# Graph attention layer on one core: where the adjacency chunks, the side jobs, the attribute sums and the projection stand in the order of a group

## The chip, the cores and the metric

The kernel runs on one NeuronCore of a Trainium2 chip. The metric is the device time of one execution in microseconds (us): the median of three runs before the change is 3267.39 us (3266.81 to 3270.06). The trace that is read here is of a separate, profiled execution.

## The reference, cut to what matters

```python
N, E = 6250, 200000                     # nodes, edges sorted by dst; 128 features, 4 heads
h  = relu(layernorm(x));  xp = h @ W
e  = leaky_relu(a_s[src] + a_d[dst]);   m = segment_max(e, dst)
w  = exp(e - m[dst])                    # softmax over the edges of a node, max subtracted
x  = x + relu(segment_sum(w/denom * xp[src], dst) + bias0)      # first layer
edge_agg = segment_sum(edge_attr @ We + be, dst)
x_comb   = concat([relu(layernorm(x)), edge_agg])
neigh    = segment_sum(x_comb[src], dst)                        # second layer
out = x + (relu((x_comb + neigh) @ W1 + b1) @ W2 + b2)
```

## The kernel before, in words

The edges are cut into 87 groups of 2304 (128 partitions x 18 columns). Every group `n` passes through an `item(n, ...)` on each of the five engines; a loop over pairs of groups runs most of them (`stage`). The items of the engines meet by semaphores only, so the order in which each engine's item is written is the order of the work.

What a group does on its main path: GpSimd (POOL) gathers the 18 columns of node rows by indirect DMA into `V` (`gather`, L906). VectorE (DVE) takes the logits, scans them (`pre1`), TensorE (PE) transposes the tails of the 128 partitions, DVE scans those (`tails`, L1835), PE brings them back (`cback`, L1298), DVE makes the running maxima and splits them into `peaks`. PE multiplies them with the group's selection matrix (`mg`, L1316: the peaks' product), DVE turns the result into the new maxima (`pen`, L1876, to `sh`), PE looks them up for every edge (`look`, L1332), DVE and ScalarE (ACT) form the weights (`lks` L1915, two exponentials), DVE multiplies the gathered rows (`vw`, L1932), and PE sums them into the window of 128 nodes (`sumV`, L1352, 36 instructions, 18 columns of two). Its last instruction signals `vm_b`; the end of it is called T in the text below. After T, SyncE (SP) may issue the attribute load of group n+2 (1152 KB) and then the load of `state`, which DVE's `rescale_state` of the next item (L1691) waits for.

Beside the main path each group has, on PE:

- `attribute_sums`: 18 columns of the edge attributes summed with the same selection in 32 bit (`SEL`, which ACT copies from the 16-bit one, `selc_b`), L1284, two instructions a column. Three columns stand ahead of the look-up, fifteen behind it.
- `adjacency`: 18 chunks of a dense adjacency for the second layer, L1253 and L1255. A chunk goes into one of three PSUM banks, and ACT copies it out into `adjE` (`keep_adjacency`, the ACTIVATE `xsb<-pt` and `xsb<-pa`, signal `ab_ev`). A chunk waits until the chunk three ahead of it has been copied out (`behind` 2 of `ab_ev`); ACT waits for PE by `ab_mm`, which is signalled for each third chunk and the last ones. When all 18 are out, SP stores 1176 KB (`store_adjacency`).
- the projection of a finished window (`transpose_window`, L1232 and L1233; ACT's copy `fhT`, `evacuate_window`; `project_window`, L1237 and L1238).
- in groups 39 to 83 a `job`: 14, 21 or 28 matmuls of 384 columns of the second layer (L1275), taken off the end of the kernel; DVE's `keep_job` (L1798) reads its result.

POOL's gather of 18 descriptors stops ahead of descriptor 11 until the peaks' product of the group before is there, and ahead of descriptor 14 until its look-up is there (`PAUSES`). Each of ACT's `keep_adjacency` calls first loads the chunks' places into registers (L1009).

PE's order in an item before the change: job part 1, tails' transpose, job part 2, `cback`, chunks 15 to 17 of group n-1, job part 3, peaks' product, chunks 0 to 2, attribute columns 0 to 2, look-up, chunks 3 to 5, attribute columns 3 to 17, transposes of window n-1, chunks 6 to 8, two thirds of `sumV`, projection of window n-1, last third of `sumV`, chunks 9 to 14. ACT's: `thruT`, chunks 15 to 17 of n-1, the copy of `SEL`, chunks 0 to 2, `fold` and the normalised window, chunks 3 to 5, the two exponentials of the weights, `fhT`, chunks 6 to 14.

Of the kernel before, what the change touches and what calls it, by code (L numbers as in the profile page):

```python
# [25 lines left out]
J = 18  # L26
# [66 lines left out]
FILL = (10, 14)  # L93


PAUSES = ((11, "mg_b"), (14, "look"))
# [19 lines left out]
def gnn_kernel(nc, x, src, dst, attr, W, att_src, att_dst, bias0, We, be, W1, b1, W2, b2, out):  # L116
    ctx = ExitStack()
    with ctx:
# [821 lines left out]
        def _(act):  # L940
# [94 lines left out]
            def item(n, b, it, like=0, is_extra=False):  # L1035
# [10 lines left out]
                if finish_before:  # L1046
                    keep_adjacency(n - 1, 1 - b, 15, 18)
# [4 lines left out]
                if not is_extra:  # L1052
                    after_dma(act, s("adj_out"), n - 1)
                    keep_adjacency(n, b, 0, 3)
                else:
# [8 lines left out]
                if not is_extra:  # L1064
                    keep_adjacency(n, b, 3, 6)
# [7 lines left out]
                if not is_extra:  # L1073
                    keep_adjacency(n, b, 6, 15)
# [5 lines left out]
            keep_adjacency(NG - 1, 0, 15, 18)  # L1080
# [41 lines left out]
        def _(pe):  # L1122
# [112 lines left out]
            def project_window(m):  # L1235
# [3 lines left out]
                if isinstance(m, int) and m == NG - 1:  # L1239
                    ins.then_inc(s("ym_f"), 1)  # L1240
# [21 lines left out]
            def job(n, like, lo, hi):  # L1262

                total = HP * parts_of(like)
                hi = min(hi, total)
                if lo >= hi:
                    return
                if lo == 0:
                    if isinstance(n, int):
                        pe.wait_ge(s("ys2"), parts_of(like))  # L1270
                    pe.wait_ge(s("aw_in"), n * 16 + (16 - JOB0 * 16))
                    pe.wait_ge(s("ab_ev"), n * J - (J - 15))
                for i in range(lo, hi):
# [3 lines left out]
                if hi == total:  # L1277
                    ins.then_inc(s("jb_mm"), 1)

            def item(n, b, it, like=0, is_extra=False):  # L1280
# [11 lines left out]
                job(n, like, 0, FILL[0])  # L1292
# [3 lines left out]
                job(n, like, FILL[0], FILL[1])  # L1296
# [3 lines left out]
                if finish_before:  # L1300
                    adjacency(n - 1, 15, 18)
# [10 lines left out]
                job(n, like, FILL[1], NB)  # L1312
# [5 lines left out]
                if not is_extra:  # L1318
                    adjacency(n, 0, 3, like)
# [4 lines left out]
                attribute_sums(0, 3)  # L1324
# [10 lines left out]
                if not is_extra:  # L1335
                    adjacency(n, 3, 6)
                attribute_sums(3, J)
# [6 lines left out]
                for q in range(QN):  # L1344
                    if q == QN - 1 and finish_before:
                        project_window(n - 1)
# [8 lines left out]
                if not is_extra:  # L1355
                    adjacency(n, 9, 15)
            stage(pe, item)
            adjacency(NG - 1, 15, 18)
# [86 lines left out]
        def _(dve):  # L1445
# [329 lines left out]
            def finish_projection(m):  # L1775

                if isinstance(m, int) and m == NG - 1:
# [307 lines left out]
```

## Time and profile before

| | us |
|---|---|
| median of 3 runs (lowest, highest) | 3267.39 (3266.81, 3270.06) |
| the profiled execution | 3249.53 |
| its span | 3247.6 |
| mean granted TensorE clock | 0.772 of full speed |
| PE busy, DVE busy, POOL busy, ACT busy | 2133.8, 1838.2, 1516.2, 1095.0 |

The span runs from the first instruction to the last one; the execution's own time lies 1.9 us above it. Groups 0 to 86 take it up to 2946.6 us, the second layer's tail the rest.

### The profile page before, as it was taken

To read this page: it belongs to the slowest core of one execution; us is meant where nothing else is said; L and a number is where in the kernel's file an instruction comes from. 1 tells how busy PE (TensorE), PEld (TensorE's weight loads), DVE (VectorE), ACT (ScalarE), POOL (GpSimd) and SP (SyncE) were. 2 spreads that over 40 slices of the span, in tenths; PEclk is the share of its full clock that TensorE was granted. 3 is DMA by queue.
4 is the path that set the end of the run, shared out by engine and by line. 5 is a ranking of instruction groups with operands and counts; after the bars stand their busy time and mean duration, and the time that the engine had idled before them with its cause. 6 is when DMAs were issued, how large, how long until landed. Compare 5 with 4: busy or idle time off the path is not lost.

```text
span 3247.6 us, 60418 instructions
## 1 busy us (share of the span) xinstructions
PE 2133.8 (66%) x16302; PEld 1640.0 (50%) x16302; DVE 1838.2 (57%) x6265; ACT 1095.0 (34%) x2343; POOL 1516.2 (47%) x1625
## 2 busy tenths in 40 slices
PE   4466665665666666656666676666676676667987
PEld 3354554554554545545445454454454445455766
DVE  7365666666666666656556565555555556564221
ACT  3333333333333344333333333333333233332000
POOL 3555555555555555554545555445444444550000
PEclk8666766766767766778878788788888788878999
DMA  9845545555555555565555655556555555655665
GB/s 195 121 137 163 167 139 163 155 153 162 155 153 163 148 165 172 152 182 150 179 153 174 173 170 180 149 162 177 159 153 176 166 147 172 180 138 189 209 198 159
DMA packets 395176, 532.44 MB, mean 164 GB/s; under 512 B 115603, under 2 KB 346723, under 8 KB 383665
## 3 DMA queue, kind: packets, MB, share of 16 engines
q1 hardware_dynamic: 344939, 415.35, 42.4%
q0 software_dynamic: 50112, 115.56, 15.9%
q8 instruction: 61, 1.00, 0.1%
q14 instruction: 64, 0.52, 0.1%
HBM read 385.48 MB, written 145.24 MB: 163 GB/s over the span
## 4 chain that ended last, share of the span: by engine, by line
PE 26%; DVE 21%; another core or an unknown queue 21%; issue 13%; DMA 8%; ACT 5%; SPq 5%; ACTq 1%; DVEq 1%
PE pv L1352 9%; PE pv L1284 5%; PE pt L1275 4%; ACT xsb L942 4%; DVE tabb L1640 4%; DMA state<-zpart 4%; DMA state<-sums 3%; PE pt L1253 2%; DVE big L1932 2%; PE pv L1409 2%; DVE lks L1915 1%; DVE fy L1759 1%; DVE fy L1768 1%; PE pt L1409 1%
## 5 line engine op out<-in xcount | busy, mean ns | idle before, releaser
L906 POOL DMA_INDIRECT big<-table,idx x1566 | 1489.2, 951 | 1372.4 <-issue 399.2
L942 ACT ACTIVATE xsb<-pt 128x343 f32 x1042 | 482.0, 463 | 1547.7 <-remote 922.0
L1253 PE MATMUL pt<-tabb 128*128 128x343 bf16 x1042 | 379.5, 364 | 448.1 <-ACT xsb L942 405.8
L1284 PE MATMUL pv<-big 128*128 128x128 f32 x3132 | 511.3, 329 | 8.0 <-issue 5.6
L1284 PEld LDWEIGHTS pv<-big 128*128 128x128 f32 x3132 | 476.3, 239 | 32.2 <-issue 13.7
L1352 PE MATMUL pv<-big 128*128 128x133 f32 x3132 | 391.6, 280 | 22.2 <-DVE big L1932 22.2
L1253 PEld LDWEIGHTS pt<-tabb 128*128 128x128 bf16 x1042 | 107.9, 104 | 553.8 <-ACT xsb L942 439.9
L1352 PEld LDWEIGHTS pv<-big 128*128 128x128 f32 x3132 | 367.9, 190 | 35.5 <-DVE big L1932 22.4
L1640 DVE TENSOR_TENSOR tabb<-pc,keyp 128x2064 bf16<-128x2064 bf16 x261 | 319.0, 1222 | 0.0
L942 ACT ACTIVATE xsb<-pa 128x343 f32 x521 | 240.9, 462 | 61.8
L1932 DVE TENSOR_TENSOR big<-big,pm 128x768 f32<-128x768 f32 x261 | 233.4, 950 | 30.8 <-ACT pm L942 19.0
L1255 PE MATMUL pt<-tabb 128*128 128x49 bf16 x1041 | 220.7, 212 | 0.0
L1691 DVE TENSOR_TENSOR state<-state,fold 128x128 f32<-128x128 f32 x87 | 25.5, 293 | 337.6 <-issue 205.1
L1253 PE MATMUL pa<-tabb 128*128 128x343 bf16 x521 | 187.3, 360 | 21.3 <-ACT xsb L942 20.6
L942 ACT ACTIVATE big<-selb 128x2304 f32<-128x2304 bf16 x87 | 183.9, 2114 | 2.6 <-issue 2.6
L1640 DVE TENSOR_TENSOR tabb<-pc,lop 128x768 bf16<-128x768 bf16 x261 | 144.3, 553 | 5.5
L1332 PE MATMUL pa<-node,selb 128*128 128x24 bf16 x1566 | 55.7, 179 | 139.5 <-DVE node L1674 59.3
L1275 PE MATMUL pt<-pro 128*128 128x384 bf16 x476 | 146.8, 492 | 0.0
L1275 PE MATMUL pt<-tabb,pro 128*128 128x384 bf16 x315 | 90.1, 447 | 84.6 <-ACT xsb L942 84.6
L1316 PE MATMUL pm<-peaks,selb 128*128 128x13 bf16 x1566 | 55.7, 173 | 122.6 <-remote 67.5
L1844 DVE SCALAR_TENSOR_TENSOR logit<-pm,cin,logit 128x4 f32<-128x4 f32 x87 | 19.3, 222 | 198.7 <-remote 180.6
L1332 PEld LDWEIGHTS pa<-node,selb 128*128 128x128 bf16 x1566 | 48.7, 101 | 158.3 <-DVE node L1674 65.3
(339 smaller groups left out, 3282.5 us busy)
## 6 DMA issues: line engine op xcount, KB each, us to landing
adj<-xsb SPq DMA_DIRECT2D x87, 1176.0 KB
big<-in_edge_attr_dram SPq DMA_DIRECT2D x87, 1152.0 KB
selb<-rel SPq DMA_DIRECT2D x87, 576.0 KB
pro<-adj SPq DMA_DIRECT2D x28, 896.0 KB
big<-table,idx POOLq DMA_INDIRECT x1566
state<-sums SPq DMA_DIRECT2D x87, 130.5 KB
sums<-state SPq DMA_DIRECT2D x87, 130.5 KB
pro<-adj SPq DMA_DIRECT2D x12, 672.0 KB
```

The lines of the kernel that those rows point to most:

```text
L906: pool.indirect_dma_start(out=V[b][:, j, 0:rows], out_offset=None, in_=table, in_offset=bass.IndirectOffsetOnAxis(ap=index[b][:, j:j + 1], ...
L942: return nc.scalar.activation(out_, in_, func, **kw).then_inc(s(name), 1)
L1253: ins = nc.tensor.matmul(to, ohl[:, c, :], ohk[:, c, 0:KW], start=True, stop=alone)
L1255: ins = nc.tensor.matmul(to.rearrange("p (q x) -> p q x", q=NPARTS)[:, :, 0:HP], ohl[:, (c - 1) % J, :], ohc[:, (c - 1) % J, 0:NB].rearran ...
L1275: ins = nc.tensor.matmul(jobP, jobT[:, q, :, h], yt[q][:, h, :], start=(i == 0), stop=(i == total - 1))
L1284: ins = nc.tensor.matmul(sumA[b], SEL[b][:, j, :], AT[b][:, j, :], start=(j == 0), stop=(j == J - 1))
L1316: ins = nc.tensor.matmul(mg, selH[:, j, :], peaks[:, j, :], start=(j == 0), stop=(j == J - 1))
L1332: ins = nc.tensor.matmul(lk[:, j, :], selT[:, j * 128:(j + 1) * 128], parts[b], start=True, stop=True)
L1352: ins = nc.tensor.matmul(sumV[b], SEL[b][:, j, :], V[b][:, j, 0:TAB], start=(j == 0), stop=(j == J - 1))
L1409: ins = nc.tensor.matmul(pay[k][0:rows, 0:NK * C], winT[k][:, q, 0:rows, h], yt[q][:, h, :], start=(i == 0), stop=(i == total - 1))
L1640: return v.tensor_tensor(to.rearrange("p j (w e) -> p j w e", e=2), v_in, at, ALU.is_equal)
L1932: v.tensor_tensor(v4, v4, wps[:, js, :].rearrange("p j (h a) -> p j h a", a=1) .to_broadcast([128, QUART, H, F]), ALU.mult).then_inc(s("vw ...
```

## The change

- `adjacency` and `keep_adjacency`: chunks 9 to 14 no longer follow `sumV`; with 15 to 17 they go into the next item, 9 to 14 behind `cback`, 15 to 17 behind the peaks' product. On ACT chunks 15 to 17 come behind the copy of `SEL`. Chunks 0 to 2 go from behind the peaks' product to behind the look-up; on ACT they stand where 3 to 5 stood, and 3 to 8 come behind `fhT`.
- `attribute_sums`: 9 columns ahead of the look-up in a group without a job, 3 in one with a job (`LEAD`), the rest behind chunks 0 to 2.
- `job`: in one piece, behind the leading attribute columns and ahead of the look-up; DVE reads it behind `edge_marks(n, 1)`.
- `project_window`: one item later, ahead of the tails' transpose; DVE's `finish_projection` waits for that transpose instead of `vm_b`.
- `PAUSES`: stops ahead of descriptors 9 and 12.

```diff
-FILL = (10, 14)
-PAUSES = ((11, "mg_b"), (14, "look"))
+PAUSES = ((9, "mg_b"), (12, "look"))
+LEAD = (9, 3)
...   ScalarE, item
                 a(thruT[:, :], thruP, ACT.Copy, "thru_c")
                 if finish_before:
-                    keep_adjacency(n - 1, 1 - b, 15, 18)
+                    keep_adjacency(n - 1, 1 - b, 9, 15)
                 after(act, s("sel_b"), n)
...
                 a(SEL[b], selH, ACT.Copy, "selc_b")
-                if not is_extra:
-                    after_dma(act, s("adj_out"), n - 1)
-                    keep_adjacency(n, b, 0, 3)
-                else:
+                if finish_before:
+                    keep_adjacency(n - 1, 1 - b, 15, 18)
+                if is_extra:
...
                 if finish_before:
                     normalise_window(n - 1)
                 if not is_extra:
-                    keep_adjacency(n, b, 3, 6)
+                    after_dma(act, s("adj_out"), n - 1)
+                    keep_adjacency(n, b, 0, 3)
...
                 if finish_before:
                     evacuate_window(n - 1)
                 if not is_extra:
-                    keep_adjacency(n, b, 6, 15)
+                    keep_adjacency(n, b, 3, 9)
...   TensorE, item
-                job(n, like, 0, FILL[0])
+                if finish_before and not (isinstance(n, int) and n < 2):
+                    project_window(n - 2)
                 after(pe, s("pre1_b"), n)
                 after(pe, s("thru_c"), n)
                 nc.tensor.transpose(tailT, ...)
-                job(n, like, FILL[0], FILL[1])
                 after(pe, s("tails_b"), n)
                 nc.tensor.matmul(cback, ...)
                 if finish_before:
-                    adjacency(n - 1, 15, 18)
+                    adjacency(n - 1, 9, 15)
...
-                job(n, like, FILL[1], NB)
                 after(pe, s("pkl_b"), n)
...
                 ins.then_inc(s("mg_b"), 1)
-                if not is_extra:
-                    adjacency(n, 0, 3, like)
+                if finish_before:
+                    adjacency(n - 1, 15, 18)
...
-                attribute_sums(0, 3)
+                lead = LEAD[1 if parts_of(like) else 0]
+                attribute_sums(0, lead)
+                job(n, like)
...   the look-up
                 ins.then_inc(s("look"), 1)
                 if not is_extra:
+                    adjacency(n, 0, 3, like)
+                if lead < J:
+                    attribute_sums(lead, J)
+                if not is_extra:
                     adjacency(n, 3, 6)
-                attribute_sums(3, J)
                 if finish_before:
                     transpose_window(n - 1)
                 if not is_extra:
                     adjacency(n, 6, 9)
                 after(pe, s("w_b"), n)
                 for q in range(QN):
-                    if q == QN - 1 and finish_before:
-                        project_window(n - 1)
...
                 ins.then_inc(s("vm_b"), 1)
-                if not is_extra:
-                    adjacency(n, 9, 15)
...   VectorE
-                    dve.wait_ge(s("vm_b"), m + 2)
+                    after(dve, s("tailT_b"), m + 2)
...
-                keep_job(n, like)
                 after(dve, s("mg_b"), n)
...
                     edge_marks(n, 1)
+                    keep_job(n, like)
                 after(dve, s("look"), n)
```

## Rows read from the trace of the kernel before

**Rows 1.** The profile's page, section 4: the chain that ended last, by engine.
```profile
PE 26%; DVE 21%; another core or an unknown queue 21%; issue 13%; DMA 8%; ACT 5%; SPq 5%; ACTq 1%; DVEq 1%
```
**Rows 2.** Windows: stretch and its length, busy us (instructions) of each engine, clock, DMA.
```profile
149.00:1316.40 1167.40, 738.30 (x5856) 591.71 (x5854) 740.26 (x2551) 456.49 (x954) 654.06 (x684) 0.68 0.55 156
1316.40:1880.60 564.20, 369.65 (x2941) 280.09 (x2940) 332.86 (x1155) 200.54 (x429) 289.39 (x306) 0.79 0.58 168
1880.60:2863.20 982.60, 657.75 (x5099) 473.48 (x5097) 550.31 (x1906) 326.69 (x700) 476.67 (x504) 0.81 0.56 164
```
**Rows 3.** Timeline, a group without a job, first part: start, us, engine, operation, idle before.
```profile
639.14 1.53 PE L1352 MATMUL pv<-big 128*128 128x133 f32 x12
...
646.43 0.25 ACT L942 ACTIVATE thruT<-pm 4x128 f32<-4x128 f32 x1
...
647.76 0.58 PE L1298 MATMUL pm<-ident,tails 4*128 4x4 f32 x2 [0.57 <-issue]
```
**Rows 4.** The same group, from the selection's copy to the look-up.
```profile
650.89 2.12 ACT L942 ACTIVATE big<-selb 128x2304 f32<-128x2304 bf16 x1
...
652.80 0.65 PE L1316 MATMUL pm<-peaks,selb 128*128 128x13 bf16 x18 [2.46 <-remote]
...
653.99 0.94 POOL L906 DMA_INDIRECT big<-table,idx  x1 [0.30 <-issue]
...
657.28 0.16 DVE L1876 TENSOR_SCALAR pen<-pm 128x1 f32<-128x1 f32 x1 [2.88 <-remote]
...
659.22 0.66 PE L1332 MATMUL pa<-node,selb 128*128 128x24 bf16 x18 [3.31 <-DVE node L1674]
```
**Rows 5.** Timeline, PE and DVE, around the peaks' product of the last group.
```profile
2933.49 0.63 PE L1316 MATMUL pm<-peaks,selb 128*128 128x13 bf16 x18 [1.17 <-DVE peaks L1676]
...
2934.36 0.15 DVE L1876 TENSOR_SCALAR pen<-pm 128x1 f32<-128x1 f32 x1
```
**Rows 6.** Timeline, a group with a job of 28.
```profile
2226.89 1.53 PE L1352 MATMUL pv<-big 128*128 128x133 f32 x12
...
2233.05 1.37 PE L1275 MATMUL pt<-tabb,pro 128*128 128x384 bf16 x7 [1.89 <-ACT xsb L942]
...
2237.65 0.32 PE L1253 MATMUL pa<-tabb 128*128 128x343 bf16 x1
...
2245.01 0.46 ACT L942 ACTIVATE xsb<-pt 128x343 f32 x1 [11.75 <-remote]
...
2245.85 4.66 PE L1275 MATMUL pt<-pro 128*128 128x384 bf16 x14
...
2252.96 0.61 PE L1332 MATMUL pa<-node,selb 128*128 128x24 bf16 x18 [0.47 <-DVE shr L1672]
...
2253.94 3.86 PE L1284 MATMUL pv<-big 128*128 128x128 f32 x30
...
2258.18 0.38 ACT L942 ACTIVATE fhT<-pa 128x256 f32<-128x256 f32 x1
```
**Rows 7.** Timeline of a group without a job, from the look-up to the end.
```profile
660.70 5.23 PE L1284 MATMUL pv<-big 128*128 128x128 f32 x30
...
666.51 2.97 PE L1352 MATMUL pv<-big 128*128 128x133 f32 x24
...
668.07 0.38 ACT L942 ACTIVATE fhT<-pa 128x256 f32<-128x256 f32 x1 [3.53 <-issue]
...
669.31 0.38 PE L1237 MATMUL pa<-w1a,fhT 128*128 128x128 f32 x2
...
669.86 1.53 PE L1352 MATMUL pv<-big 128*128 128x133 f32 x12
...
670.39 0.47 ACT L942 ACTIVATE xsb<-pt 128x343 f32 x1 [1.94 <-issue]
```
**Rows 8.** ScalarE's register loads of the chunks' places: min/median/max ns.
```profile
L1009 ACTq TENSOR_LOAD <-offs x347: 15/711/2864, 128.6 to 2941.6; - x174
```
**Rows 9.** Windows of the group without a job, columns as in rows 2.
```profile
644.00:660.00 16.00, 6.82 (x63) 4.22 (x62) 8.04 (x47) 7.14 (x14) 10.16 (x11) 0.50 0.65 186
```

More of the change, by code:

```diff
@@ L1079, in _ @@
             stage(act, item)
-            keep_adjacency(NG - 1, 0, 15, 18)
+            keep_adjacency(NG - 1, 0, 9, 18)
             normalise_window(NG - 1)
@@ L1238, in project_window @@
                 ins = nc.tensor.matmul(finY, fhT[:, C:2 * C], wew[:, :], start=False, stop=True)
-                if isinstance(m, int) and m == NG - 1:
+                if isinstance(m, int) and m >= NG - 2:
                     ins.then_inc(s("ym_f"), 1)
@@ L1260, in adjacency, with job @@
                         ins.then_inc(s("ab_mm"), 1)
-            def job(n, like, lo, hi):
+            def job(n, like):
                 total = HP * parts_of(like)
-                hi = min(hi, total)
-                if lo >= hi:
+                if not total:
                     return
[L1268 to L1273, printed above, removed]
+                if isinstance(n, int):
+                    pe.wait_ge(s("ys2"), parts_of(like))
+                pe.wait_ge(s("aw_in"), n * 16 + (16 - JOB0 * 16))
+                pe.wait_ge(s("ab_ev"), n * J - (J - 15))
+                for i in range(total):
                     q, h = divmod(i, HP)
@@ L1276, in job @@
                                            stop=(i == total - 1))
[L1277 to L1278 removed]
+                ins.then_inc(s("jb_mm"), 1)
             def item(n, b, it, like=0, is_extra=False):
@@ L1354, in item @@
                 ins.then_inc(s("vm_b"), 1)
-                if not is_extra:
-                    adjacency(n, 9, 15)
             stage(pe, item)
-            adjacency(NG - 1, 15, 18)
+            project_window(NG - 2)
+            adjacency(NG - 1, 9, 18)
             transpose_window(NG - 1)
@@ L1775, in finish_projection @@
             def finish_projection(m):
-                if isinstance(m, int) and m == NG - 1:
-                    dve.wait_ge(s("ym_f"), 1)
+                if isinstance(m, int) and m >= NG - 2:
+                    dve.wait_ge(s("ym_f"), m - (NG - 3))
                 else:
-                    dve.wait_ge(s("vm_b"), m + 2)
+                    after(dve, s("tailT_b"), m + 2)
                 dve.wait_ge(s("y_out"), m * 16 + 16)
```

## The prediction
> **What bounds the kernel now.** I read the windows of the three kinds of groups first, then one group of each kind in the timeline, then the last group, which has no successor.
>
> The windows give the periods [rows 2]. Groups 1 to 38 (no job) take 1167.40 / 38 = 30.72 us each, groups 39 to 55 (14 or 21 job matmuls) 564.20 / 17 = 33.19, groups 56 to 83 (28) 982.60 / 28 = 35.09. No engine is busy for much over two thirds of any of them, and the chain that ended last is spread over PE, DVE and a fifth of unexplained time [rows 1]. So a group is one serial loop, from the end of one `sumV` (T) to the end of the next, and what counts is what stands on it.
>
> In the group without a job T is 639.14 + 1.53 = 640.67 [rows 3]. The tails come back at T+7.1. The peaks' product starts at T+12.1 and is done at 12.8, but DVE reads it at T+16.6 [rows 4]. In the last group, where POOL gathers nothing, the same read comes 0.24 after the product's end [rows 5]. So signals from PE are held in a stretch of the group, and something else than the product sets T+16.6. The job group shows the same edge: its T is 2228.42, chunk 16 of the group before is done at T+9.6, and ACT copies chunk 15 only at T+16.6 after 11.75 us of idling [rows 6]. What both have in common is POOL's eleventh descriptor, which ends at T+14.3 [rows 4], 2.3 ahead of the release.
>
> From there the loop is short. The look-up starts at T+18.55 [rows 4], `sumV` at T'-4.88 = 666.51, that is 7.29 after the look-up at 659.22, and T' = 669.86 + 1.53 = 671.39 is 12.17 after it [rows 7].
>
> **The change part by part**, with T for the end of the `sumV` before and L for the start of the look-up.
>
> *The projection* leaves the middle of `sumV`. From its first row at 669.31 to the last third of `sumV` at 669.86 are 0.55 us of PE on the loop, some 0.1 of it the transposed `thru` that stays [rows 7]. Ahead of the tails they lie in PE's idle time while DVE waits for `state`. Gain 0.45 a group. The wait that DVE gets instead of `vm_b` is for a transpose that it waits for anyway: 0.
>
> *Chunks 9 to 14 behind `cback`.* ACT's `thruT` is no longer behind nine copies, but DVE cannot scan tails before `rescale_state`, so I count nothing for that (at most the 0.5 between the two). Behind `cback` (T+7.1 to 7.4) chunks 9, 10, 11 go to PE at once and ACT copies them, 0.47 and some 0.1 between them, so 0.58 each (an estimate from [rows 7]); chunks 12 to 14 follow as the banks come free, the last at about T+10.1. ACT waits for its signal before it copies 12, then come three copies (1.75), then the copy of `SEL`, 2.12 [rows 4], which before started at T+10.2. If that signal is only little late (arrival T+11.6), `SEL` is copied from 13.5 to 15.6. Bounds: signal at once, 14.1; signal held to the release, 20.5.
>
> *Chunks 15 to 17 behind the product.* This is a new wait with a queue behind it. Chunk 17 needs chunk 15 copied out, ACT copies 15 only after `SEL`, and behind chunk 17 on PE stand the attribute columns, the job and the look-up. Chunk 16 is sent at about T+13, in the held stretch, so chunk 15 is copied at the release or after `SEL`, whichever is later.
>
> *The stops.* With a stop ahead of descriptor 9 instead of 11, the last descriptor before it ends 2 x 1.25 earlier. Whether the release follows is not in the trace; the bounds are T+14.1 and T+16.6. I take the earlier one, since the one group without gathers has no hold [rows 5]. A later end of the gather costs nothing: six descriptors behind the look-up are 7.5 us, against a remaining 12 and more.
>
> So chunk 15 is copied at about T+15.7 to 16.1 and chunk 17 done at T+16.5.
>
> *Attribute columns.* Nine ahead of the look-up are 18 instructions. Thirty take 5.23 us here [rows 7] and 3.86 in the job group [rows 6], 0.17 and 0.13 each, so 2.3 to 3.1 us. Without a job L = 16.5 + 2.8 = T+19.3 against 18.55: loss 0.75. Bounds: T+17.3 (every signal prompt, full clock) and 24.3 (hold as now and catching chunk 14).
>
> *The job.* Its 28 matmuls stood half ahead of `cback`, partly hidden, and half ahead of the product, 4.66 us bare [rows 6]. Now all are bare ahead of L. At the low clock one is 4.66 / 14 = 0.33, at the high one half of it: ten low, eighteen high are 6.3. L = 16.5 + 1.0 (three columns) + 6.3 = T+23.8 against 2252.96 - 2228.42 = 24.54 [rows 6]: gain 0.75. Bounds 20.3 and 31. With 14 or 21 (mean 19) 4.8, L = 22.3 against about 22: loss 0.3. `keep_job` (0.56 on DVE) lies in the wait for the look-up: 0.
>
> *Behind the look-up* is the dearest part. PE's order still has chunks 6 to 8 ahead of `sumV`. Chunk 6 needs chunk 3 copied out, chunk 8 chunk 5. Before, ACT copied 3 to 5 ahead of the weights; now it copies them behind both exponentials and behind `fhT`, which waits for PE's transposes. So `sumV` waits for transposes, `fhT`, the places' load and three copies. Step by step, no job: chunks 0 to 2 and 18 attribute instructions, chunk 5 at L+5.3 (ACT's copies of 0 to 2 pace it), transposes done at L+5.6; `fhT` at L+5.9 if their signal is prompt, as in the job group, 2258.18, at L+5.2 [rows 6], or L+8.2 if it is 2.3 late, as here, where `fhT` starts at 668.07 with the transposes long over [rows 7]. From `fhT` to the first copy it is 670.39 - 668.07 = 2.32 with nine places; three places load in 0.7 [rows 8], so six are about 1.65. Copy of 3 at L+7.55, of 4 and 5 by L+9.2, chunk 8 by L+9.35, `sumV` without the projection 4.43 to 4.65: T' = L+14.0. Before 12.17: loss 1.8 (upper bound 4.1, with the late `fhT`). With a job of 28, PE has 30 attribute instructions there (at 0.13) and comes to the same point at about L+14.2. Before, such a group ended 35.09 - 24.0 = 11.1 after its look-up (mean period of rows 2, less the mean start of the look-up, which in the group read is T+24.5 of 35.6): loss 3.1.
>
> *The sum.* No job: 0.75 + 1.8 = 2.6 a group, 40 groups (1 to 38, 84, 85): 104. Groups 39 to 55: (0.3 + 3.1) x 17 = 58. Groups 56 to 83: (3.1 - 0.75) x 28 = 66. Together 228, on the profiled execution's 3249.5 us: 3477. The median of the runs is 17.9 above that execution, so about **3490** (rounded to the nearest ten).
>
> The clock is a further cost, not in the sum. From T+3.3 to T+19.3 it is granted at 0.50, the low level of 1.2 GHz, with PE busy 6.82 of 16 us [rows 9]. The change puts a gap of some 3.5 us on PE right ahead of `sumV`. The Trainium skill (TensorE: Matmul & The Clock Gate, "HAM oscillation") says that idle gaps between bursts of matmuls drop the clock so that the next burst starts slow; by that rule some of `sumV`'s 36 instructions would run at half rate, up to 4 us more a group. The rows agree that the level falls behind idle stretches; that it would fall in this one, they don't show.
>
> **The rivals.**
>
> *A, the release stays at T+16.6*, whatever POOL does. For it: it is the same in a group with and one without a job, though their stores and products lie elsewhere. Chunk 15 is then copied from T+16.6 instead of about 15.7, chunk 17 is done 1.0 later, and with it every L. 85 x 1.0 more: 3477 + 85 + 18 = 3580.
>
> *B, the hold catches chunk 14's signal too.* For it: in the job group a signal sent at T+9.6 was held to the end [rows 6]. Against: here the three copies of chunks 15 to 17 and `SEL` went on until T+10.2 [rows 4]. Copies from T+14.1, `SEL` to 18.0, chunk 17 at 18.9, everything 2.4 later: 85 x 2.4 = 204 more, 3700.
>
> *C, faster: fewer descriptors in flight take the hold away altogether*, at the peaks and at the look-up, as in the last group [rows 5]. Then `SEL` is done at T+14.1, chunk 17 at 14.9, PE is at the high level, and the weights come 1.3 earlier. No job: L = 17.3, T' = L+12.7 = 30.0, gain 0.7. Groups 39 to 55: 14.9 + 0.8 + 3.2 + 12.9 = 31.8, gain 1.4. Groups 56 to 83: 14.9 + 0.8 + 4.6 + 12.9 = 33.2, gain 1.9. 28 + 24 + 53 = 105 off: 3163. It decides from the point where chunk 17 is done before T+15.6 and `fhT` starts within 0.3 of the transposes; either alone is not enough. On the rule that DMAs of SP and POOL share the same engines and interleave (Trainium Kernel Development and Optimization, "Key Constraints") it is possible; no row here shows the share that the gathers have in the hold.
>
> **How the numbers follow.** Forecast 0.38, A 0.25, B 0.15, C 0.12, and 0.10 for small outcomes between C and the forecast, of which 0.03 within 0.2% of before. A measurement of this kernel can tell about 0.2%, 6.5 us. Range: C is left out below and part of B above; it begins where the small losses do, 3275, and ends at 3715. Forecast's own range 3420 to 3540. Slower 0.85, same 0.03, faster 0.12.
>
> **What would show it.** In the changed kernel's timeline: PE idle ahead of chunk 6, released by ACT's copy of chunk 3, and `sumV` starting 9.3 behind the look-up instead of 7.3; PE idle ahead of chunk 17, released by ACT's copy behind `SEL`; DVE's read of the product at T+14.1 (or 16.6, A); no projection between the parts of `sumV`. I am wrong if `fhT` and the copies of 3 to 5 are out before the weights are, if attribute columns start before T+16, or if the period without a job is under 30.7.

## The result, and the profile after

The changed kernel takes 3990.64 us (median, 3986.23 to 3991.74) against 3267.85 (3266.81 to 3270.06) for the kernel before on the same chip: 1.2208 times as long, 95% interval 1.2187 to 1.2229. Forecast was 3490 with a range of 3275 to 3715. The direction was right; the loss is 723 us instead of 223.

The profiled execution after has a span of 3987.7 us. First its page: the chain of waits by engine, then of the costliest groups those that have changed (busy time, mean ns, idle time before and what ended most of it).

```profile
PE 34%; issue 23%; another core or an unknown queue 17%; ACT 11%; ACTq 7%; DMA 4%; DVE 2%; SPq 1%; DVEq 0%
...
L1251 PE MATMUL pt<-tabb 128*128 128x343 bf16 x1042 | 431.3, 414 | 926.7 <-ACT xsb L940 760.0
L940 ACT ACTIVATE xsb<-pt 128x343 f32 x1042 | 481.3, 462 | 1698.9 <-PE pt L1253 799.4
...
L1349 PE MATMUL pv<-big 128*128 128x133 f32 x3132 | 519.5, 337 | 0.0
...
L940 ACT ACTIVATE fhT<-pa 128x256 f32<-128x256 f32 x87 | 33.3, 383 | 437.4 <-remote 424.9
```

DVE has all but gone from the chain (2%, 21% before) and ACT has come in [rows 1]. PE waits 760 us for ACT's copies of adjacency chunks, and ACT waits 425 us for a signal ahead of `fhT` (`issue` and the unknown queue together have grown from 34% to 40%). The windows of the same three kinds of groups, columns as in [rows 2]:

```profile
152.70:1603.50 1450.80, 798.03 (x5851) 619.06 (x5851) 739.84 (x2550) 445.55 (x954) 651.41 (x684) 0.68 0.45 126
1603.50:2343.90 740.40, 419.85 (x2942) 312.81 (x2942) 338.35 (x1160) 200.95 (x429) 292.18 (x306) 0.70 0.44 128
2343.90:3587.10 1243.20, 708.05 (x5099) 531.32 (x5098) 554.22 (x1904) 325.65 (x700) 477.80 (x504) 0.73 0.44 129
```

The periods are 1450.80 / 38 = 38.18 us without a job (30.72 before), 740.40 / 17 = 43.55 with 14 or 21 products (33.19) and 1243.20 / 28 = 44.40 with 28 (35.09).

In the timeline of a group without a job, T is 535.74 + 0.39 = 536.13 and L 557.55. From the tails to the look-up, where [rows 3, 4] stood before:

```profile
545.75 0.46 ACT L940 ACTIVATE xsb<-pt 128x343 f32 x1
...
546.26 0.47 PE L1251 MATMUL pt<-tabb 128*128 128x343 bf16 x1
...
546.98 0.95 POOL L904 DMA_INDIRECT big<-table,idx  x1 [0.30 <-issue]
...
549.92 0.48 ACT L940 ACTIVATE xsb<-pt 128x343 f32 x1 [3.72 <-remote]
550.03 0.16 DVE L1871 TENSOR_SCALAR pen<-pm 128x1 f32<-128x1 f32 x1 [0.83 <-remote]
...
551.45 2.11 ACT L940 ACTIVATE big<-selb 128x2304 f32<-128x2304 bf16 x1
...
553.96 0.47 PE L1251 MATMUL pt<-tabb 128*128 128x343 bf16 x1 [2.42 <-ACT xsb L940]
...
557.55 0.60 PE L1328 MATMUL pa<-node,selb 128*128 128x24 bf16 x18
```

Chunk 14 (the row at 546.26) is done at T+10.6, and ACT copies chunk 12, which waits for it, only at T+13.8, together with DVE's read of the product at T+13.9. `SEL` is copied from T+15.3, chunk 17 starts at T+17.8, the look-up at T+21.4. Behind it, for [rows 7]:

```profile
561.28 0.27 PE L1231 MATMUL pa<-ident,state 128*128 128x128 f32 x1
...
564.67 0.38 ACT L940 ACTIVATE fhT<-pa 128x256 f32<-128x256 f32 x1 [3.84 <-remote]
566.37 0.46 ACT L940 ACTIVATE xsb<-pt 128x343 f32 x1 [1.31 <-issue]
566.88 0.47 PE L1251 MATMUL pt<-tabb 128*128 128x343 bf16 x1 [5.33 <-ACT xsb L940]
...
568.46 3.92 PE L1349 MATMUL pv<-big 128*128 128x133 f32 x24
...
572.32 1.53 PE L1349 MATMUL pv<-big 128*128 128x133 f32 x12
```

PE stands 5.33 us ahead of chunk 6, for the chain transposes, `fhT`, load of places, copy of chunk 3; `fhT` begins 3.1 us behind the transposes' end. A group with 28 products (T = 2522.4) shows more of it, for [rows 6]:

```profile
2542.00 1.96 PE L1271 MATMUL pt<-tabb,pro 128*128 128x384 bf16 x7
...
2547.21 0.60 PE L1328 MATMUL pa<-node,selb 128*128 128x24 bf16 x18
...
2552.40 0.27 PE L1231 MATMUL pa<-ident,state 128*128 128x128 f32 x1
...
2557.30 0.38 ACT L940 ACTIVATE fhT<-pa 128x256 f32<-128x256 f32 x1 [6.72 <-remote]
...
2559.48 0.47 PE L1251 MATMUL pt<-tabb 128*128 128x343 bf16 x1 [6.81 <-ACT xsb L940]
```

Here the transposes' signal takes 4.6 us to reach ACT. And `sumV` itself is slower. Its window in the kernel before (first line), then in the kernel after, where the third number from the end is the granted clock:

```profile
666.51:671.39 4.88, 4.88 (x45) 4.78 (x43) 4.73 (x10) 1.26 (x3) 1.01 (x2) 1.00 0.12 30
```
```profile
568.46:573.85 5.39, 5.39 (x41) 5.36 (x40) 3.72 (x7) 1.38 (x3) 0.00 (x0) 0.82 0.00 0
```

### The profile page after: what moved, and what is told of

Read it like the earlier page. It is cut to its first block, busy times and chain, and to the rows that moved or that the text cites. A ratio compares the mean times of both kernels' runs of the same rounds, so it can differ in the third digit from the quotient of the medians.

```text
span 3987.7 us, 60478 instructions
## 1 busy us (share of the span) xinstructions
PE 2301.5 (58%) x16302; PEld 1763.0 (44%) x16302; DVE 1846.4 (46%) x6265; ACT 1082.4 (27%) x2343; POOL 1517.2 (38%) x1625
## 4 chain that ended last, share of the span: by engine, by line
PE 34%; issue 23%; another core or an unknown queue 17%; ACT 11%; ACTq 7%; DMA 4%; DVE 2%; SPq 1%; DVEq 0%
PE pv L1349 12%; ACT xsb L940 9%; PE pv L1279 6%; PE pt L1271 5%; ACTq L1007 5%; PE pt L1251 4%; DMA state<-zpart 3%; PE pv L1405 1%; ACTq L940 1%; PE pa L1328 1%; DMA state<-sums 1%; PE pa L1251 1%; DVE cols L1983 1%; ACT big L940 1%
## 5 line engine op out<-in xcount | busy, mean ns | idle before, releaser
L1251 PE MATMUL pt<-tabb 128*128 128x343 bf16 x1042 | 431.3, 414 | 926.7 <-ACT xsb L940 760.0
L1349 PE MATMUL pv<-big 128*128 128x133 f32 x3132 | 519.5, 337 | 0.0
L1349 PEld LDWEIGHTS pv<-big 128*128 128x128 f32 x3132 | 505.1, 248 | 14.1
L1279 PEld LDWEIGHTS pv<-big 128*128 128x128 f32 x3132 | 462.7, 234 | 16.8
L1293 PE MATMUL pm<-ident,tails 4*128 4x4 f32 x174 | 50.5, 358 | 509.1 <-issue 455.4
L1293 PEld LDWEIGHTS pm<-ident,tails 4*128 4x128 f32 x174 | 42.9, 304 | 528.0 <-issue 471.8
L1251 PE MATMUL pa<-tabb 128*128 128x343 bf16 x521 | 216.5, 416 | 14.5 <-issue 1.6
L1794 DVE TENSOR_REDUCE tabb<-pt 128x128 f32<-128x384 f32 x45 | 25.1, 558 | 290.0 <-PE pt L1271 290.0
L940 ACT ACTIVATE fhT<-pa 128x256 f32<-128x256 f32 x87 | 33.3, 383 | 437.4 <-remote 424.9
L1911 DVE TENSOR_REDUCE lks<-pa 128x144 f32<-128x432 f32 x87 | 52.4, 603 | 173.9 <-PE pa L1328 173.9
L940 ACT ACTIVATE thruT<-pm 4x128 f32<-4x128 f32 x87 | 23.2, 266 | 374.1 <-PE pv L1349 338.9
```

Source lines behind the costliest of these rows:

```text
L940: return nc.scalar.activation(out_, in_, func, **kw).then_inc(s(name), 1)
L1251: ins = nc.tensor.matmul(to, ohl[:, c, :], ohk[:, c, 0:KW], start=True, stop=alone)
L1279: ins = nc.tensor.matmul(sumA[b], SEL[b][:, j, :], AT[b][:, j, :], start=(j == 0), stop=(j == J - 1))
L1293: nc.tensor.matmul(cback, tails[:, 0:128], ident[0:H, 0:H], start=True, stop=True)\
L1349: ins = nc.tensor.matmul(sumV[b], SEL[b][:, j, :], V[b][:, j, 0:TAB], start=(j == 0), stop=(j == J - 1))
L1911: v.tensor_reduce(lks[:, :, :].rearrange("p j (g h) -> p (j g) h", h=H), lk.rearrange("p j (g k h) -> p (j g) h k", k=NK, h=H), AX.X, ALU. ...
```

## The experiments

The runs fell on several chips, and these are of two kinds. On some, the kernel before takes 3247 to 3268 us; on the others the same kernel takes 2621 to 2650. So each kernel is told by its ratio to the kernel before on its own chip, and the kinds are called "with hold" and "without hold", for the reason that the third series gives. The table has means over the groups of a kind, worked out from the traces of all 38 (no job) and 28 (28 products) groups; DVE's read of the product and L are counted from T. What was expected in us of m1 to m4, which ran without hold, was written for a chip with it and is held against ratios or differences.

```
kernel                           ratio (95%)             no job: read     L  T'-L period | 28: period
WITH HOLD
before                           1                              16.57 18.52 12.20  30.72 |      35.09
after                            1.221 (1.219 to 1.223)         13.85 21.68 16.50  38.18 |      44.40
s1 before, new stops             0.971 (0.970 to 0.973)         13.90 15.87 13.61  29.48 |      34.03
s2 s1 and projection             0.974 (0.973 to 0.976)         14.32 16.86 12.68  29.54 |      34.00
s5 before, stops 7 and 10        0.972 (0.969 to 0.975)         12.32 14.35 15.98  30.33 |      32.60
s3 after, old stops              1.236 (1.234 to 1.238)         16.50 23.68 16.28  39.96 |      44.04
s4 after, 9-14 undone            1.167 (1.165 to 1.169)         13.72 18.47 17.29  35.76 |      42.87
u4 s4, 6-8 behind, job back      1.022 (1.019 to 1.026)         17.28 22.43  9.63  32.06 |      34.94
WITHOUT HOLD
c1 before                        1.000 (0.998 to 1.002)         11.31 13.59 11.05  24.64 |      25.58
c2 after                         1.316 (1.310 to 1.321)         11.35 19.07 13.89  32.96 |      37.24
c3 before, new stops             0.999 (0.997 to 1.000)         11.29 13.55 11.12  24.67 |      25.42
b1 c3, 6-8 behind sumV           1.049 (1.047 to 1.052)         12.60 14.99 10.64  25.63 |      28.01
c4 as m1                         1.146 (1.140 to 1.151)         11.42 19.00  8.71  27.71 |      32.36
m4 c3, segment alone             1.231 (1.226 to 1.236)         11.30 13.60 18.40  32.00 |      32.67
m1 after, 6-8 behind sumV        1.140 (1.135 to 1.145)         11.51 19.08  8.71  27.79 |      32.35
m2 m1 and marks later            1.141 (1.136 to 1.146)         13.22 19.11  8.76  27.87 |      32.43
m3 after, SEL first              1.245 (1.239 to 1.251)         11.41 17.73 13.64  31.37 |      34.86
u1 after, 9-14 undone, 6-8 beh.  1.105 (1.101 to 1.108)         12.51 17.67  8.82  26.49 |      30.78
u2 u1, 15-17 undone              1.099 (1.096 to 1.102)         12.57 17.41  8.90  26.31 |      30.76
u3 u2, three columns ahead       1.100 (1.097 to 1.103)         12.84 15.27 11.08  26.35 |      30.76
```

### The stops, alone and undone

s1 is the kernel before with one line changed; s3 is the changed kernel with it changed back.

```diff
-PAUSES = ((11, "mg_b"), (14, "look"))
+PAUSES = ((9, "mg_b"), (12, "look"))
```

> The kernel before with nothing changed but the stops (descriptors 9 and 12 instead of 11 and 14). Theory: the held signals are let go 2.2 to 2.5 us behind the last descriptor ahead of the stop, so DVE reads the peaks' product at T+14.1 instead of T+16.6, the look-up starts at T+16.1 to 16.5, and the six descriptors behind it cost at most a part of that: 1 to 2.5 us a group off, 3060 to 3180 us. Rival: the release moved in the changed kernel for another reason (its store of the adjacency sums or its loads lie elsewhere): DVE reads at T+16.6 as before and the time is 3268 within 0.3%.

> The changed kernel with the stops back at 11 and 14. Theory: release back at T+16.6, and copies of chunks 12 to 14, SEL, chunk 17 and the look-up all 2.5 us later: 85 x 2.5 = 213 more than the changed kernel, about 4200. Rival (the stops don't set the release): 3990 within 20.

s1 takes 3160.74 against 3255.0, s3 4021.33. DVE's read moves from T+16.57 to 13.90 and back to 16.50: the stops set it, in both kernels. Both rivals fall. But in s1 the 2.7 us come out as 1.24 a group, and of the expected 213 us in s3 there are 31 (49 by the ratios). With 28 products the look-up of s3 is 2.55 later than in the changed kernel (T+27.35, 24.80), but T'-L is 2.9 shorter (16.69, 19.60): two descriptors fewer follow the look-up, and `fhT` starts at L+7.2 instead of 10.1. In s1 the look-up starts 2.65 earlier and what is behind it takes 1.4 longer. Its timeline, behind a look-up at 461.43, shows why: six descriptors follow a second stop there instead of four.

```profile
468.55 0.31 PE L1253 MATMUL pt<-tabb 128*128 128x343 bf16 x1
...
471.54 0.95 POOL L906 DMA_INDIRECT big<-table,idx  x1 [0.30 <-issue]
...
473.21 0.56 DVE L1640 TENSOR_TENSOR tabb<-pc,lop 128x768 bf16<-128x768 bf16 x1 [2.13 <-remote]
473.79 1.31 PE L1352 MATMUL pv<-big 128*128 128x133 f32 x10 [0.91 <-issue]
```

Chunk 8 is done at 468.9, DVE sees it at 473.2, 0.7 us after the last descriptor's end. So there is a second hold, behind the look-up, and it grows with the descriptors that are left for it: T'-L is 12.20 with four, 13.61 with six. s5 goes on the same way (7 and 10).

> The kernel before with the stops earlier still, at descriptors 7 and 10. Theory (the release follows the last descriptor ahead of the stop): on a chip with the hold DVE reads the product at T+12 to 13.5, now set by the product itself, look-up 0.5 to 1.8 earlier than with stops at 9 and 12: 0.94 to 0.965 of before; eight descriptors behind the look-up and three ahead of it end 2.5 us later in the group, and the next group's first read of the gathered rows becomes late on a chip without the hold: 1.00 to 1.04 there. Rival (the release has another floor): 0.97 with the hold, as with 9 and 12.

```profile
466.11 0.65 PE L1316 MATMUL pm<-peaks,selb 128*128 128x13 bf16 x18 [1.49 <-DVE peaks L1676]
467.24 0.15 DVE L1876 TENSOR_SCALAR pen<-pm 128x1 f32<-128x1 f32 x1
...
481.27 0.27 PE L1352 MATMUL pv<-big 128*128 128x133 f32 x1 [0.90 <-issue]
482.70 0.38 PE L1352 MATMUL pv<-big 128*128 128x133 f32 x1 [1.16 <-issue]
484.13 1.94 PE L1352 MATMUL pv<-big 128*128 128x133 f32 x8 [1.05 <-issue]
```

3157.34 against 3247.01. The read is as early as the theory had it, 0.48 behind the product, and all further gain is lost again, now inside `sumV`, which breaks up into pieces (T'-L 15.98, with eight descriptors behind the look-up). The expected 0.94 to 0.965 was missed; the rival's number came in, for another reason than the rival's.

### The projection

> The same stops and the projection ahead of the tails, on the kernel before. Theory: another 0.45 us a group off against the stops alone, 85 x 0.45 = 38 us. Rival: the projection's matmuls warm PE's clock for sumV's end and their going costs as much as it gives: the same as the stops alone within 10 us.

s2 adds the projection ahead of the tails (its diff is that part of the change). 3168.06 (3152.24 to 3183.59), nothing gained against s1: the rival's number, but not its reason, since `sumV` is shorter (5.94 instead of 6.66). Behind the look-up it does save 0.93 (13.61 to 12.68), but the tails' scan, at T+6.27 without a job and 8.66 with one, comes at 6.73 and 10.39. There the projection is not hidden: with 28 products the transpose that the scan waits for ends 0.8 later, and the scan starts 1.05 behind it instead of 0.11.

### What the hold is worth, and what it is not

In the second series, m1 to m4, the kernel before took 2650 us. So before, after, s1 and m1 were run together:

> The kernel before, unchanged, profiled on the chip on which the others of this series run. The first series ran where it takes 3255 us, the second where it takes 2650. Theory: the whole difference is the hold of PE's and DVE's signals, which a chip has or has not: where it is missing, DVE reads the product within 0.3 us of its end and the period without a job is under 26 us. Rival: the chip without it moves data faster: then the gathers' 1.25 us each and the loads differ too.

> The changed kernel unchanged, in the same series. Theory: the loss lies in waits of the changed order and not in the hold alone, so the ratio to before is 1.2 or more on either kind of chip: 3970 to 4000 where before takes 3260, 3250 to 3400 where it takes 2650. Rival (the hold makes the loss): a ratio under 1.08 on a chip without it.

> The kernel before with the new stops. Theory: they gain only where there is a hold for them to shorten: 0.971 of before on a chip with it, 1.00 (0.99 to 1.01) without. Rival (they help in another way too): 0.97 on both.

> The changed kernel with chunks 6 to 8 behind sumV. It had 1.14 of before's time where before took 2650. Theory (the wait of sumV is the greatest loss on either kind of chip): 0.08 of before's time less than the changed kernel in this series, so with the hold 3560 to 3720, without it 3018. Rival (with the hold, sumV's own signals are late): 3850 or more on a chip with it.

Medians 2620.22, 3450.10, 2617.30 and 3005.99 (1.146) against 2621.55. The kernel before, here:

```profile
569.91 0.65 PE L1316 MATMUL pm<-peaks,selb 128*128 128x13 bf16 x18 [0.78 <-DVE peaks L1676]
...
570.89 0.15 DVE L1876 TENSOR_SCALAR pen<-pm 128x1 f32<-128x1 f32 x1
```

The read comes 0.33 behind the product (0.42 in the mean) and not 3.8 [rows 4]. The gather descriptors take the same (961 ns mean against 955), as do the copy of `SEL` (2.12) and `sumV`. The rival, that this chip moves data faster, falls too: loads of 672 KB land in 4.4 us here and in 4.5 there, and `state` is there at T+5.9 in both. What differs is how late the signals are. The stops gain nothing here; the rival that they help in another way falls. And the changed kernel loses more, 829 us, a ratio of 1.316 where 1.2 or more was expected (in us it is above the 3250 to 3400). c4 is 0.170 of before's time below c2, twice the expected 0.08. So the loss doesn't need the hold: the order of the work makes it without one. In the same place of the changed kernel:

```profile
498.26 0.38 ACT L940 ACTIVATE fhT<-pa 128x256 f32<-128x256 f32 x1 [0.76 <-PE pa L1231]
...
500.46 0.47 PE L1251 MATMUL pt<-tabb 128*128 128x343 bf16 x1 [2.24 <-ACT xsb L940]
...
502.04 5.50 PE L1349 MATMUL pv<-big 128*128 128x133 f32 x24
```

`fhT` follows the transposes at once, and PE still idles 2.24 us ahead of chunk 6, as the forecast's chain had it.

### Chunks 6 to 8 ahead of sumV

```diff
                 if finish_before:
                     transpose_window(n - 1)
-                if not is_extra:
-                    adjacency(n, 6, 9)
...
                 ins.then_inc(s("vm_b"), 1)
+                if not is_extra:
+                    adjacency(n, 6, 9)
```

> The changed kernel with the places of chunks 6 to 8 alone moved from ahead of sumV to behind it; ACT's copies and DVE's marks stay. Theory (sumV waits for chunks 6 to 8, which wait for fhT and ACT's copies): sumV starts 2 us behind the first product of values by weights, at L+5.2 instead of L+10.8 to 12.4, 5 us a group of it; DVE's next marks and ACT's thruT now wait for chunk 8 behind sumV, which gives some 1.5 us back: 86 x 3.5 to 5 = 300 to 430 off, 3560 to 3690. Rival (sumV is late for its own signals, held by the gathers behind the look-up): sumV starts no earlier than L+9 and the time is above 3850.

m1 takes 3017.85, and 3005.99 as c4. c4 is 444 us or 5.2 a group below c2, which was run with it: just above what the theory had. The rival could not be tried here, since it speaks of held signals. It has two halves: `sumV` starts 3.7 earlier (L+4.25 instead of 7.93), and takes 4.46 instead of 5.96. First PE ahead of `sumV` in m1, then the windows of `sumV` in m1 and in c2:

```profile
446.87 0.27 PE L1231 MATMUL pa<-ident,state 128*128 128x128 f32 x1
447.29 2.99 PE L1347 MATMUL pv<-big 128*128 128x133 f32 x24 [0.15 <-DVE big L1928]
```
```profile
447.29:451.76 4.47, 4.47 (x39) 4.38 (x40) 3.50 (x5) 1.65 (x4) 3.51 (x4) 1.00 0.28 67
```
```profile
502.04:509.01 6.97, 6.97 (x41) 6.94 (x40) 3.78 (x7) 1.38 (x3) 0.75 (x1) 0.63 0.08 21
```

Without the gap PE is granted 1.00 through `sumV`, with it 0.63 in this group and 0.74 in the mean of the 38. The 1.5 us a group that DVE's wait was to give back were not seen: the time is that of the kernel with the marks moved as well.

```diff
+                if not is_extra:
+                    edge_marks(n, 0)
                 after(dve, s("mg_b"), n)
...
                     edge_marks(n, 2)
-                    if not (isinstance(n, int) and n == NG - 1):
-                        edge_marks(n + 1, 0)
```

> The same, and the marks for chunks 0 to 5 of the next group made inside that group, ahead of DVE's read of the product, so that DVE doesn't wait for chunk 8. Theory: the 1.5 us a group that the wait gives back are kept: 3480 to 3560. Rival (DVE's wait costs nothing, the tails wait for something else): the same as the kernel with chunks 6 to 8 behind sumV alone, within 20 us.

3021.09: the rival is right, DVE's marks lie in its wait for `state` (the tails' scan is at T+6.3 in both). The same one edit on the kernel before does not help, though:

> The kernel before with the new stops and one thing of its own: chunks 6 to 8 placed behind sumV instead of ahead of it. Theory (PE's places ahead of sumV are what made it start 2 to 3.2 us behind the first product of values by weights; behind it they lie where PE waits for the tails): 1 to 1.5 us a group less than with the stops alone, so a ratio to before of 0.93 to 0.945 on a chip with the hold (0.971 with the stops alone), 0.95 to 0.965 on one without (0.9985). Rival (DVE's marks for the next group, which wait for chunk 8, are then late and delay the tails): no gain or a loss against the stops alone.

2758.2 against 2627.86, 0.051 worse than the stops alone; the rival's outcome. In a group with a job (T = 1742.2):

```profile
1748.48 0.46 ACT L942 ACTIVATE xsb<-pt 128x343 f32 x1
1748.84 0.25 ACT L942 ACTIVATE thruT<-pm 4x128 f32<-4x128 f32 x1
1748.99 2.45 PE L1275 MATMUL pt<-tabb,pro 128*128 128x384 bf16 x7 [1.85 <-ACT xsb L942]
...
1752.72 0.41 DVE L1833 TENSOR_TENSOR_SCAN tails<-thruT,pm 4x128 f32<-4x128 f32 x1 [4.51 <-PE pm L1295]
```

Not DVE's marks, as the rival said, but ACT's nine copies (6 to 14) and behind them the job's first products now stand ahead of the tails, T+10.5 instead of 7.7. Where `sumV` ends and the tails begin, three more chunks on ACT are on the loop.

### The part alone, and the parts undone one behind the other

m4 puts on the kernel before (new stops) only the order behind the look-up: `adjacency(n, 0, 3)` behind it, `keep_adjacency(n, b, 0, 3)` behind the exponential of `fold`, `keep_adjacency(n, b, 3, 15)` behind `fhT`.

> The kernel before with the new stops (3161 us) and one part of the change alone: chunks 0 to 2 behind the look-up, ACT's copies of 3 to 14 behind both exponentials and fhT. Theory (this part is the dearest): sumV starts at L+11 and more instead of L+6.7 to 7.7, 3.5 to 5 us a group more: 3460 to 3590. Rival (it only costs together with the late copies of 9 to 17): under 3300. The forecast's own figure for this part, 1.8 to 3.1 us a group, would give 3370.

3258.69, 0.232 more than c3, 7.3 us a group without a job: more than the theory's 5. Here twelve places are loaded ahead of the first copy, which starts 2.9 us behind `fhT` (2.3 with nine places, 1.65 with six), and `sumV` starts at L+11.9.

m3, then s4, on the changed kernel (what is left out of s4's diff is the last group's):

```diff
-                if finish_before:
-                    keep_adjacency(n - 1, 1 - b, 9, 15)
                 after(act, s("sel_b"), n)
...
                 a(SEL[b], selH, ACT.Copy, "selc_b")
                 if finish_before:
+                    keep_adjacency(n - 1, 1 - b, 9, 15)
                     keep_adjacency(n - 1, 1 - b, 15, 18)
```
```diff
                 a(thruT[:, :], thruP, ACT.Copy, "thru_c")
-                if finish_before:
-                    keep_adjacency(n - 1, 1 - b, 9, 15)
...
-                    keep_adjacency(n, b, 3, 9)
+                    keep_adjacency(n, b, 3, 15)
...
                     .then_inc(s("cback_b"), 1)
-                if finish_before:
-                    adjacency(n - 1, 9, 15)
...
                 ins.then_inc(s("vm_b"), 1)
+                if not is_extra:
+                    adjacency(n, 9, 15)
```

> The changed kernel with ACT's copy of SEL ahead of its copies of chunks 9 to 14. Theory (the copies of 12 to 14 are held to the release at T+13.8 and SEL and chunk 17 queue behind them): chunk 17 done at T+16.3 instead of 17.9, look-up 1.6 earlier, 85 x 1.6 = 136 off, 3855. Rival (the gathers behind the look-up take back what is won ahead of it): look-up earlier, sumV not, within 40 us of 3990.

> The changed kernel with one part undone: chunks 9 to 14 behind sumV again, their copies ahead of thruT. Theory (the held signal of chunk 14 costs 2.4 us a group, the segment behind the look-up the rest): SEL copied ahead of the release, chunk 17 done near T+16, look-up at T+19.3 instead of 21.8 without a job; twelve places instead of six are loaded behind fhT, so 0.7 us given back: 85 x 1.7 = 145 off, 3845. Rival (nearly all of the loss is behind the look-up): look-up earlier, but sumV no earlier: within 40 us of 3990. Second rival (the held signal is nearly all of it): 3500 or less.

3294.84 (0.071 below c2) and 3796.76 (0.054 below after). Both start the look-up earlier, by 1.3 and 3.2; the queue of copies, `SEL`, chunk 17 is on the loop with and without the hold. The rival of m3 again needs a chip with the hold. s4 loses 0.8 of it again behind the look-up, where twelve places are loaded, and is still 48 us under the 3845 of its theory; both of its rivals fall.

u1 is s4 with chunks 6 to 14 behind `sumV` (`adjacency(n, 6, 15)`, and none ahead of it). u2 and u3 go on from it:

```diff
                     .then_inc(s("cback_b"), 1)
+                if finish_before:
+                    adjacency(n - 1, 15, 18)
...
                 ins.then_inc(s("mg_b"), 1)
-                if finish_before:
-                    adjacency(n - 1, 15, 18)
...
+                if finish_before:
+                    keep_adjacency(n - 1, 1 - b, 15, 18)
                 after(act, s("sel_b"), n)
```
```diff
-LEAD = (9, 3)
+LEAD = (3, 3)
```

> The changed kernel with two parts undone or eased: chunks 9 to 14 behind sumV as before, and 6 to 8 behind it too. Theory (the losses add up: 9 to 14 some 0.055 of before's time, 6 to 8 some 0.17): a ratio of 1.00 on a chip with the hold, 1.04 to 1.08 on one without. Rival (they share one wait, so the second undone gives little): above 1.09 on either.

> The same, and chunks 15 to 17 back behind cback with their copies ahead of SEL's. What is left of the change: the projection, 0 to 2 behind the look-up, the job behind the attribute columns, nine of those without a job, the stops. Theory (chunk 17 behind the product delays columns, job and look-up by 1 to 2 us): 0.04 to 0.07 less than the kernel before it in this series. Rival (the look-up waits for the nine columns, 2.8 us): under 0.02 less.

> The same, and three attribute columns ahead of the look-up in all groups. Theory: without a job the twelve instructions that go behind it free 1.0 to 1.9 us ahead of it and lie behind it in a wait for the weights: 40 x 1 to 1.9 = 40 to 76 us less (0.012 to 0.028). Rival (they then stand ahead of the transposes and sumV, and nothing is won): within 0.005.

u1 2902.22, u2 2886.46, u3 2889.26. With 6 to 8 out of the way, undoing 9 to 14 gives 0.036 (m1 1.140 to u1 1.105) and the ratio is above the rival's 1.09: they do not add up, since the tails slip from T+6.3 to 7.6. Here the place of 15 to 17 is worth 0.006 and the nine columns nothing (both times the rival was right): L is 2.1 earlier with three, T'-L 2.2 longer. More than half of what is left in u3 is in the groups with 28 products: 30.76 against 25.58 in c1, that is 28 x 5.2 = 145 us of its 261. Without a job a group is 1.7 longer than in c1 (26.35 against 24.64).

u4 is u1 with the job's three calls of before:

```diff
+                job(n, like, 0, FILL[0])
                 after(pe, s("pre1_b"), n)
...
+                job(n, like, FILL[0], FILL[1])
                 after(pe, s("tails_b"), n)
...
+                job(n, like, FILL[1], NB)
                 after(pe, s("pkl_b"), n)
...
                 attribute_sums(0, lead)
-                job(n, like)
```

> The changed kernel with chunks 9 to 14 and 6 to 8 behind sumV (as in the series before) and the job's products back in their three places ahead of the peaks' product. Groups without a job are those of that kernel, groups with one show the job. Theory: a moved job costs 2.5 to 4 us a group where the product is read at once (a ratio of 1.06 to 1.075 on a chip without the hold, against 1.105 with the job moved), and about nothing where the product is held anyway (a ratio of 0.99 to 1.01 on a chip with it); in groups without a job on a chip with the hold the period falls from 35.9 (chunks 6 to 8 ahead of sumV) to 31 or 32. Rival (the job was hidden in neither): 1.10 on a chip without the hold.

u4, on a chip with the hold, 3327.17. Where nothing of the job is in play, T'-L falls from 17.3 (s4) to 9.6; half of that is given back, L being 4.0 later, because `fhT` is held, the twelve copies behind it start at T+0.9, `thruT` follows them, and the tails come at T+12.6 in the group read (11.7 in the mean):

```profile
470.44 0.24 ACT L941 ACTIVATE thruT<-pm 4x128 f32<-4x128 f32 x1
```
```profile
473.56 0.41 DVE L1833 TENSOR_TENSOR_SCAN tails<-thruT,pm 4x128 f32<-4x128 f32 x1 [5.30 <-remote]
```

(T = 461.0.) With 28 products the period falls from 42.87 to 34.94 by both edits together; their shares on such a chip are not told apart. The expected 31 to 32 us without a job came in (32.06), the ratio of 0.99 to 1.01 was missed by 0.01. What the expectation asked of a chip without the hold, the cost of the moved job alone, no run shows.

**The version to keep** is s1, the kernel before with the new stops: 0.971 with the hold, and the same as the kernel before without it (0.999, 0.997 to 1.000). s5 is level with it on the first kind of chip and was not run on the second.

## Why the prediction was right in direction and far too low

*The loop from T to T' and what stands on it*: right. The period is L plus T'-L by definition; what the runs add is that every queue that was moved changed L, T'-L or both.

*The release moves with the stops*: right, T+13.85 where 14.1 was forecast. Rival A is refuted by s1 and s3. Rival C, that the hold goes with fewer descriptors in flight, too: it moves behind the look-up (s1, s5). But the sentence beside it, "A later end of the gather costs nothing", failed: s1 loses 1.4 us behind the look-up by it, and the changed kernel, against s3, 0.2, 2.9 and 2.9 in the three kinds of groups, 139 us, a part of the 348 below.

*The signal of chunk 14 arrives at T+11.6*: this step failed. It arrives at T+13.8, with the release. That is rival B's mechanism, given 0.15. `SEL` and chunk 17 come 1.8 us late; the look-up without a job is at T+21.68 instead of 19.3. With 28 products it is only 1.0 late (24.80 for 23.8), since the job took 5.3 us and not 6.3. Over all groups 40 x 2.38 + 17 x 1.26 + 28 x 1.0 = 145 us. The forecast's own price for B, 3700, was too low as well: the greater part of the loss lies behind the look-up.

*Behind the look-up, T' = L+14.0 to 14.2*: this step failed by more. The chain was the right one and so was its middle: `fhT` to first copy 1.65, as forecast. But I took `fhT` as prompt at L+5.9, behind transposes done at L+5.6. The transposes are done at L+4.2 and, with a job, 5.5, and `fhT` starts at L+6.9 and 10.1: 2.75 and 4.6 us late, where I had set 2.3 as the upper bound. Measured T'-L is 16.50, 20.00 and 19.60 where 14.0, 14.3 (33.19 + 3.4 - 22.3) and 14.2 were forecast: 40 x 2.5 + 17 x 5.7 + 28 x 5.4 = 348 us, 70% of what was missing. That T'-L without a job is 13.9 in c2, close to the 14.0, is luck: there `fhT` is early, at L+4.3, and `sumV` takes some 1.4 longer than forecast. In both failed steps a signal that PE sends while POOL issues descriptors was taken at its prompt end although [rows 6] had one held for 7 us, and the new order makes such a signal gate the loop twice where it had gated it once.

*The clock*, named and left out of the sum: it belonged in it. `sumV` takes 5.87 us without a job instead of 4.89, though the projection's 0.45 has left it, so 1.4 us (1.9 and 1.4 with a job); about 130 us, and a part of the 348. Through `sumV` the mean granted clock is 1.00 before, 0.75 in the changed kernel without a job (groups from 0.62 to 0.82), 0.74 in c2, and 1.00 in m1, where the gap is gone. The trace agrees in kind with what the Trainium skill says of idle gaps between bursts (TensorE: Matmul & The Clock Gate, "HAM oscillation"). The length of the gap alone doesn't tell the cost: c2's is 2.2 us against 4.9 in the changed kernel, for the same clock without a job, and with 28 products, behind the same 2.2, some groups of c2 are at 1.00.

*The projection gains 0.45*: not seen. Ahead of the tails it is hidden in the changed kernel, as forecast: they are at T+6.2, when `state` is there, and were at 6.4. But the slower clock takes more from `sumV` than the projection gave. In s2, where the copies of 9 to 14 and the job stand ahead of the tails too, it isn't hidden.

*The columns and the job*: the columns do cost ahead of the look-up, as forecast, and are without worth in total (u3). The job was forecast to gain 0.75 in full groups; the look-up is 0.85 later there (T+23.95 before, 24.80 after). What the move alone costs is not shown. Without the hold it is at most the 5.2 us a group that are left in u3, and a group without a job has 1.7 left there. With the hold part of the job was on the loop before as well (L is 5.4 later with 28 products than without a job, against 1.8 in c1), so there was less to lose by moving it.

*The arithmetic* has two slips, both small. For 28 products L was compared with the 24.54 of the group read and T'-L with a mean start of 24.0, which leaves out 28 x 0.54 = 15 us; and 3477 + 17.9 is 3495, which rounds to 3500.

## What to carry to other kernels

Before an instruction is put behind another engine's result, write down every queue that the result has passed: here PE's last stretch before `sumV` came to wait for PE, ACT, a load of registers and ACT again. If the trace shows one signal arriving late in a stretch, price every signal that the new order sends in that stretch at the latest that the rows show (7 us were in them, 2.3 were set), and add the clock that the resulting gap takes away. And an edit that gains on one stretch of a serial loop is only told by the period: s2, s5 and u3 won 0.9 to 2.1 us in one stretch and lost it again in another.

## What the runs showed of the hardware

In three of the series the kernel before took 2621 to 2650 us, in the three others 3247 to 3268, each series on one chip. Instruction times agree (a gather descriptor 0.96 us, the copy of `SEL` 2.12, `sumV` 4.88). The difference is in signals between engines while POOL issues gather descriptors: 0.04 us (the transposes in c2) to 0.4 (the product in c1) on the one kind; 3.1 (chunk 14), 4.3 (chunk 8 in s1) and 4.6 (the transposes with a job) on the other. Ahead of the stop they are let go some 2 us behind the last descriptor (546.98 + 0.95 = 547.93 to 549.92), and moving the stop by two descriptors, 2.5 us, moves that by 2.65. What in the chip does this, and what tells the kinds apart, is open: of the gathers these runs change nothing but the descriptors' places, and no run changes the chip alone.
